# A transformer kernel on one core: another written order at attention's end and through the first two feed-forward samples

## What is computed

```python
h = layernorm(x, gamma1, beta1)
Q = (h @ Wq + bq).reshape(B, T, N_HEADS, D_HEAD).transpose(0, 2, 1, 3)
...
scores = jnp.einsum('bhqd,bhkd->bhqk', Q, K) / np.sqrt(D_HEAD)
scores = jnp.where(causal, scores, -jnp.inf)
attn = jax.nn.softmax(scores, axis=-1)
...
attn_out = ctx @ Wo + bo
x1 = x + attn_out
h2 = layernorm(x1, gamma2, beta2)
ff = jax.nn.gelu(h2 @ W1 + b1, approximate=False) @ W2 + b2
x2 = x1 + ff
g = gate_score[:, None, None]
return x + g * (x2 - x)
```

## Time and profile before

| | |
|---|---|
| median of 3 runs | 1648.11 us (1647.98 to 1650.59) |
| the profiled execution | 1649.63 us, its span 1647.8 us |
| TensorE busy | 1596.5 us, 97% of the span |
| VectorE, ScalarE, GpSimd busy | 1166.0, 980.5, 397.2 us |
| mean granted clock of TensorE | 0.985 of full speed |

### The profile page before, as it was taken

How to read it: one execution, slowest core, us unless ns; L and a number is a source line. 1 busy time by engine, 2 the same in 40 slices (tenths; PEclk the granted TensorE clock), 3 DMA queues, 4 the chain that set the end, 5 groups by cost and what they waited for, 6 DMA issues and landing times.

```text
span 1647.8 us, 27195 instructions
## 1 busy us (share of the span) xinstructions
PE 1596.5 (97%) x9318; PEld 1312.3 (80%) x9318; DVE 1166.0 (71%) x2767; ACT 980.5 (60%) x2329; POOL 397.2 (24%) x606
## 2 busy tenths in 40 slices
PE   5799999999999999999999989999999999999999
PEld 3678777777777777777777668888999999999898
DVE  6799887896868686868678366676565656565643
ACT  5689764987878787878788545343342424242422
POOL 6788800413131313131311110101001020202010
PEclk8999998999999999999999899999999999999999
DMA  7112224544444444444346351866555555646451
GB/s 304 74 77 78 102 91 115 159 115 115 113 120 112 121 112 121 117 116 117 91 98 199 124 220 58 326 238 233 213 205 211 190 219 175 260 151 251 168 205 71
DMA packets 61826, 254.80 MB, mean 155 GB/s; under 512 B 10581, under 2 KB 15957, under 8 KB 45945
## 3 DMA queue, kind: packets, MB, share of 16 engines
q1 hardware_dynamic: 61688, 253.06, 47.1%
HBM read 153.93 MB, written 48.23 MB: 123 GB/s over the span
## 4 chain that ended last, share of the span: by engine, by line
PE 85%; DVE 5%; DMA 4%; ACT 2%; POOL 2%; issue 1%; SPq 1%; DVEq 0%; ACTq 0%; POOLq 0%
PE psum L83 22%; PE psum L84 22%; PE psum L85 21%; PE psum L1647 5%; PE psum L1667 5%; PE psum L1697 4%; DMA k_raw<-in_w_in 1%; DMA k_early<-in_w 1%; PE psum L1588 1%; PE psum L1596 1%; PE psum L1578 1%; PE psum L2597 1%; PE psum L1683 0%; DMA out<-k_result 0%; DMA k_stack<-k_maxima 0%
## 5 line engine op out<-in xcount | busy, mean ns | idle before, releaser
L1347 ACT ACTIVATE psum<-psum,b_mx 128x512 f32<-128x512 f32 (+3 forms) x512 | 258.9, 508 | 64.6 <-DVE b_mx L1094 63.1
L1094 DVE CUSTOM_DVE_ANT_0 psum<-psum,b_mask 128x512 f32<-128x512 f32 (+3 forms) x512 | 244.6, 506 | 54.1 <-PE psum L1647 48.8
L2543 ACT ACTIVATE k_act<-k_stack_f,k_smalls 128x512 f32<-128x512 f32 x112 | 81.0, 723 | 336.1 <-DVE k_stack_f L2381 336.1
L1359 ACT ACTIVATE k_exps<-psum 128x512 f32<-128x512 f32 (+1 forms) x384 | 195.1, 531 | 62.2 <-PE psum L1667 59.5
L968 POOL TENSOR_SCALAR_AFFINE_SELECT k_exps<-k_exps 128x256 f32<-128x256 f32 x256 | 97.2, 417 | 385.8 <-ACT k_exps L1359 385.8
L2360 DVE TENSOR_TENSOR k_act_lo<-k_act,k_act_hi 128x512 fp32r<-128x512 f32 x112 | 77.4, 691 | 130.5 <-ACT k_act_hi L2546 130.5
L2241 POOL TENSOR_SCALAR k_result<-k_result,k_pb 128x512 f32<-128x512 f32 x32 | 58.4, 1840 | 433.5 <-DVE k_result L2300 433.5
L83 PE MATMUL psum<-k_act_hi,k_w_hi 128*128 128x512 f32 x384 | 152.0, 396 | 2.0 <-DVE k_act_lo L2353 1.5
L84 PE MATMUL psum<-k_act_lo,k_w_hi 128*128 128x512 f32 x384 | 151.6, 395 | 0.0
L85 PE MATMUL psum<-k_act_hi,k_w_lo 128*128 128x512 f32 x384 | 151.2, 394 | 0.0
L2381 DVE TENSOR_TENSOR k_raw<-psum,k_raw 128x256 f32<-128x256 f32 x168 | 70.7, 421 | 105.4 <-PE psum L85 99.1
(11 more groups left out here) (377 smaller groups left out, 4411.7 us busy)
## 6 DMA issues: line engine op xcount, KB each, us to landing
k_stack<-w_factors SPq DMA_DIRECT2D x35, 1792.0 KB, 7.9
k_stack<-k_samples SPq DMA_DIRECT2D x384, 128.0 KB, 2.4
k_weights<-w_factors SPq DMA_DIRECT2D x17, 1792.0 KB, 7.7
x<-k_tokens SPq DMA_DIRECT2D x10, 1024.0 KB, 3.9
k_tokens<-x SPq DMA_DIRECT2D x8, 1024.0 KB, 5.3
d<-k_result SPq DMA_DIRECT2D x32, 256.0 KB, 2.9
k_raw<-x SPq DMA_DIRECT2D x8, 1024.0 KB, 4.9
k_raw<-d SPq DMA_DIRECT2D x8, 1024.0 KB, 7.0
```

Source lines behind the costliest of these rows:

```text
L1094: last = dve.tensor_tensor_reduce(got, got, mask[:, S - width:S], -INV_SQRT_DH, -2.0 * MASKED, ALU.add, ALU.min, mx[n % 2][:, h, t:t + 1])
L1347: act.activation(sc(n, u)[:, at:at + width], sc(n, u)[:, at:at + width], ACT.Exp, bias=mx[n % 2][:, h, t:t + 1], scale=-1.0, accum_out=sum ...
L1359: act.activation(exps[n % 2][:, h, at:at + width], by_key(n, u)[:, 0:width], ACT.Exp, scale=INV_SQRT_DH).then_inc(k_act, 1)
L2543: act.activation(act_f[:], whole_tile, ACT.Gelu, bias=small(smalls, "b1", 2 * pair % M + second)).then_inc(pair_gelu, 1)
```

## The change

The four tail functions of SP, VectorE, ScalarE and TensorE get another order. They now reach through sample 1 as well (all of its eight pairs, with pair 8's products, the first of sample 2), so that `samples()` begins with sample 2. The same calls are made with the same arguments. GpSimd's order stays. No wait is added inside a call; only places change. SP's part in full, of the others the pieces at which the text looks (`partial_of`, `finish` and the like of sample 1 are now written in the tail, before they came from `period`):

```diff
 def sync_tail(att, ff):
     att.first_after()
     att.max_rows(29, 1)
     att.stack_rows(31, (0, 1))
+    ff.second_weights(0)
     att.max_rows(30, 0)
     att.attention_out(6, 0)
+    att.stack_rows(31, (2, 3))
+    att.max_rows(30, 1)
     att.attention_out(6, 1)
-    att.stack_rows(31, (2, 3))
     ff.first_weights(0)
-    ff.second_weights(0)
-    att.max_rows(30, 1)
+    att.attention_out(6, 2)
     att.max_rows(31, 0)
-    att.attention_out(6, 2)
+    att.max_rows(31, 1)
+    ff.first_weights(1)
     att.attention_out(6, 3)
-    att.max_rows(31, 1)
     ff.second_weights(1)
     att.attention_out(7, 0)
-    ff.first_weights(1)
-    for k in range(1, 4):
-        att.attention_out(7, k)
     ff.second_weights(2)
+    att.attention_out(7, 1)
+    att.attention_out(7, 2)
     ff.pair_in(2)
+    att.attention_out(7, 3)
     ff.sample_in(1)
+    ff.second_weights(3)
+    ff.pair_in(3)
     ff.factors_out(2)
-    ff.pair_in(3)
-    ff.second_weights(3)
     ff.pair_in(0)
     ff.factors_out(3)
     ff.pair_in(1)
     ff.factors_out(0)
     ff.pair_in(4)
     ff.factors_out(1)
+    ff.factors_in(2)
+    ff.pair_in(5)
+    ff.sample_out(0)
+    ff.factors_out(4)
+    ff.factors_in(3)
+    ff.sample_in(2)
+    ff.factors_in(4)
+    ff.pair_in(6)
+    ff.factors_out(5)
+    ff.factors_in(5)
+    ff.pair_in(7)
+    ff.factors_out(6)
+    ff.factors_in(8)
+    ff.factors_out(7)
...
         def samples():
-            factors_in(2)
-            factors_in(3)
-            pair_in(5)
-            factors_out(4)
-            sample_out(0)
-            factors_in(4)
-            sample_in(2)
-            pair_in(6)
-            factors_out(5)
-            factors_in(5)
-            pair_in(7)
-            factors_out(6)
-            factors_in(HALF)
-            factors_out(7)
             for n in range(HALF + 1, HALF * (B - 1)):
...
 def vector_tail(att, ff):
...
     ff.split(0)
-    ff.w1_low(2)
     att.attention_result(7, 0)
     ff.w2_low(1)
+    att.attention_result(7, 1)
+    ff.split(1)
+    ff.w1_low(2)
+    att.attention_result(7, 2)
     ff.w2_low(2)
-    att.attention_result(7, 1)
-    att.attention_result(7, 2)
-    ff.w2_low(3)
+    ff.w1_low(3)
     att.attention_result(7, 3)
-    ff.split(1)
+    ff.split(2)
     ff.start_result(0)
...
 def scalar_tail(att, ff):
...
+    ff.w2_high(0)
     att.ctx_high(30)
-    att.exponentials_by_key(31, 6)
-    att.exponentials_by_key(31, 7)
-    ff.w1_high(1)
-    ff.w2_high(0)
-    for k in range(8, 12):
+    for k in range(7, 12):
         att.exponentials_by_key(31, k)
     ff.w2_high(1)
+    ff.w1_high(1)
     ff.w2_high(2)
     ff.gelu(0)
...
         def samples():
-            period(0, HALF - 1)
-            for b in range(1, B):
+            for b in range(2, B):
                 for p in range(HALF):
                     period(b, p)
```

More of the change, by code:

```diff
@@ L2706, in samples @@
         def samples():
-            period(0, HALF - 1)
-            for b in range(1, B):
+            for b in range(2, B):
                 for p in range(HALF):
                     period(b, p)
-        return steps(tokens, back, first_product, second_product, samples)
+        return steps(tokens, back, spread, first_product, second_product, product, samples)
     return {"sync": sync, "gpsimd": gpsimd, "vector": vector, "scalar": scalar, "tensor": tensor}
@@ L3092, in vector_tail @@
     att.maxima_out(31, 1)
-    for k in range(3):
+    ff.w1_low(0)
+    for k in range(1, 4):
         att.split_low(k, 8)
-    ff.w1_low(0)
-    att.split_low(3, 8)
     att.ctx_low(30)
@@ L3171, in vector_tail @@
     ff.block_low(1, 2)
+    ff.w2_low(15)
     ff.split(14)
+    ff.split(15)
     ff.block_low(1, 4)
-    ff.factor_low(1, 3)
-    ff.w2_low(15)
-    ff.split(15)
+    ff.factor_low(4, 0)
+    ff.partial_of(0, 0)
+    ff.partial_of(0, 1)
+    ff.factor_low(4, 1)
+    ff.factor_sums(4)
+    for k in range(2, 5):
+        ff.partial_of(0, k)
+    ff.pair_low(0, True)
+    ff.partial_of(1, 0)
+    ff.factor_low(4, 2)
+    ff.finish(0, 0)
+    ff.finish(0, 1)
+    ff.factor_low(4, 3)
+    ff.finish(0, 2)
@@ new lines, in vector_tail @@
+    ff.finish(0, 3)
+    for k in range(1, 4):
+        ff.partial_of(1, k)
+    ff.pair_low(0, False)
+    ff.partial_of(1, 4)
+    ff.partial_of(2, 0)
+    ff.partial_of(2, 1)
+    ff.pair_low(1, True)
+    ff.start_result(1)
+    ff.factor_low(5, 0)
+    ff.factor_low(5, 1)
+    ff.pair_low(1, False)
+    ff.partial_of(2, 2)
+    ff.partial_of(2, 3)
+    ff.factor_sums(5)
+    ff.partial_of(2, 4)
+    ff.partial_of(3, 0)
+    ff.pair_low(2, True)
+    ff.factor_low(5, 2)
+    ff.factor_low(5, 3)
@@ new lines, in vector_tail @@
+    ff.partial_of(3, 1)
+    ff.pair_low(2, False)
+    ff.add_attention(2)
+    ff.partial_of(3, 2)
+    ff.partial_of(3, 3)
+    ff.factor_low(6, 0)
+    ff.pair_low(3, True)
+    ff.partial_of(3, 4)
+    ff.statistics(2, 0)
+    ff.statistics(2, 1)
+    ff.partial_of(4, 0)
+    ff.factor_low(6, 1)
+    ff.factor_sums(6)
+    ff.partial_of(4, 1)
+    ff.statistics(2, 2)
+    ff.pair_low(3, False)
+    for k in range(2, 5):
+        ff.partial_of(4, k)
+    ff.statistics(2, 3)
+    ff.pair_low(4, True)
@@ new lines, in vector_tail @@
+    ff.factor_low(6, 2)
+    ff.partial_of(5, 0)
+    ff.factor_low(6, 3)
+    ff.centre(2)
+    ff.pair_low(4, False)
+    for k in range(1, 4):
+        ff.partial_of(5, k)
+    ff.factor_low(7, 0)
+    ff.normalise(2)
+    ff.partial_of(5, 4)
+    ff.factor_low(7, 1)
+    ff.partial_of(6, 0)
+    ff.pair_low(5, True)
+    ff.partial_of(6, 1)
+    ff.factor_sums(7)
+    ff.block_low(2, 0)
+    ff.partial_of(6, 2)
+    ff.partial_of(6, 3)
+    ff.factor_low(7, 2)
+    ff.block_low(2, 5)
+    ff.pair_low(5, False)
@@ L3179, in scalar_head @@
+    ff.pair_low(8, True)
+    ff.partial_of(8, 4)
 def scalar_head(mod, att):
@@ L3833, in tensor_tail @@
+    att.score_by_key(31, 7)
     ff.first_product(0)
@@ new lines, in tensor_tail @@
+    ff.second_product(22, 7, 2, 3)
+    ff.tokens(2, 2)
+    ff.product(4, 5)
+    ff.product(4, 2)
+    ff.product(4, 3)
+    ff.second_product(23, 6, 0, 1)
+    ff.tokens(2, 3)
+    ff.product(5, 1)
+    ff.product(5, 6)
+    ff.second_product(23, 6, 2, 3)
+    ff.spread(2)
+    ff.product(5, 7)
+    ff.product(5, 4)
+    ff.product(5, 5)
+    ff.second_product(24, 9, 0, 1)
+    ff.second_product(24, 9, 2, 3)
+    ff.product(5, 2)
+    ff.product(5, 3)
+    ff.product(6, 1)
+    ff.product(6, 6)
```

575 lines of the change are left out of this document (369 added, 206 removed).

## The result

The changed kernel takes 1630.07 us (median of 4 runs, 1629.38 to 1630.64), the kernel before 1648.05 beside it (1646.33 to 1650.59): a ratio of 0.9889, 95% interval [0.9872, 0.9907]. The forecast was 1632 within 1626 to 1643. The profiled execution has a span of 1628.8 us.

The account below looks back on a forecast made before the run. TensorE, busy 97%, was taken to bound the kernel, with 23.3 us to be had. Terms 5 + 10 + 2 - 1 = 16 us off the 1647.8 us span gave 1631.8, as a median 1632 us, range 1626 to 1643.

Parts of the forecast that it names:

- What bounds the kernel: TensorE, busy 97% of the span; only its idle time and low clock in three stretches, 23.3 us, could be won.
- First stretch: Attention's end, 900 to 920 us: earlier maxima rows end the stop and clock fall; 5 us, between 1.5 and 8.6.
- the delay of the W2 quarter: Attention's end: the W2 quarter, issued earlier, delays group 30's first maxima; taken as zero, up to 2 us.
- rival B: Attention's end: ScalarE or the W2 quarter holds it, low clock returns, nothing gained there; 1637 or 1642 us, chance 0.20.
- no stop at k_maxima: Sign of being right, 900 to 920 us: TensorE no longer waits for maxima; clock above 0.9, under 2 us idle.
- the walk: Step-by-step timing of the new order, with moved transfers and engine work, to see which stops go and what becomes late.
- the rest: 840 to 900 us and places not walked: reshuffling there can only lose, 0 to 3 us, taken as 1.
- Second stretch: First feed-forward products, 950 to 984 us: earlier transfers and low halves end stops and clock fall; 10 us, bounds 5 and 10.3.
- 0.3 us at the tokens: First feed-forward products: sample 1's load becomes late for TensorE's transposes, the tightest place; taken as 0.3, from 0 to 3 us.
- Third stretch: Pairs of sample 1, 1060 to 1120 us: earlier output store, later result start; 2 us, from 4.3 to a loss of 5.
- Rival D: Sample 1 onward: factor load 4 over 5 us late makes later loads late; slower, 1655 us, chance 0.06.
- Rival C: SP's in-order queue: a held issue holds small transfers behind it, stops return one place later; 1645 to 1651 us, chance 0.06.

Follow-up runs that it names:

- maxima_first: Kernel before, with only the maxima rows of group 30's second half issued ahead of half of W1 and a quarter of W2; 1642.16 us, measured once.
- w1_early: Kernel before, with only the second half of W1 issued earlier, right behind group 31's maxima and ahead of the result stores; 1650.72 us, measured once.
- three_moves: Kernel before, with three SP moves: group 30's second maxima and W1's second half earlier, last W2 quarter with pair load 3 before the first factor store; 1636.44 us.
- third_new: Kernel before, with the new order only through sample 1, from the first pair product on; 1644.72 us, ratio 0.9980.
- third_sp_old: Changed kernel, with SP's order through sample 1 put back as before; 1629.27 us, ratio 0.9893.
- sp_all: Kernel before, with the whole of SP's new order, through sample 1, other engines in their old order; 1634.73 us, ratio 0.9925.
- sum_later: Changed kernel, with group 29's second maxima issued ahead of the 2 MB load and VectorE's first_sum(0) moved later; 1633.64 us, ratio 0.9921.
- sp_new: Kernel before, with SP's new order alone up to the last factor store of sample 0; 1637.24 us, ratio 0.9943.
- heads_old: Changed kernel, with VectorE, ScalarE and TensorE in the old order through attention's end and sample 0; 1631.85 us, ratio 0.9909.
- sp_old: Changed kernel, with SP's old order up to the last factor store of sample 0; 1648.89 us, ratio 1.0005.

## Why the prediction was right, point by point

**What bounds the kernel.** Right: 20.65 us came off TensorE's idle and busy time in the pieces around the three named stretches, of the 23.3 that could be had, and the 500.75 us behind them did not move. That the time came within 2 us of 1632 is in part luck: the terms made 16 us and the pieces 20.65, M came 1.65 us later, and the median lies 1.3 us over the profiled span, not the 0.3 that the forecast added.

**First stretch, 5 us taken, 4.80 measured, but made otherwise.** The transfer was the right one: maxima_first shows that its move alone makes the gain. How it delays was misread: the rows did not need 12.71 us to issue, but 2.57, and then waited behind 3 MB (in the first section). Taking the delay of the W2 quarter as zero held: no stop of TensorE answers to it. What was wrong is how the 5 us were made up. I took them from ScalarE's load (3.2 at 83% busy, 6.9 never idle) and counted idle time and clock alike; in fact 4.07 are clock and 0.73 idle. Little of the idle time was given back: 1.85 of 4.31 us stayed in 900 to 920, and a stop of 1.74 us came at 883. ScalarE is busy 20.97 us of 23.60 (89%), above the 83% that I allowed it. It is what was late next, as forecast, if only by little: TensorE's stop of 0.50 us at 907.75 is for its copy (k_tokens), and the one of 0.96 us at 910.45 for maxima that VectorE could not finish before ScalarE's logarithms:

```profile
910.04 0.36 DVE L1174 TENSOR_TENSOR b_mx<-b_mx,b_logs 128x8 f32<-128x8 f32 x1 [1.24 <-ACT b_logs L1392]
```

These stops did not bring the low clock, and so rival B's first half falls. The sign that I named, "no stop at k_maxima", holds in 900 to 920, for which it was named; the one that is left is group 29's, 20 us earlier, and the walk had not looked there. That is where "the rest" of -1 us went: 2.10 - 0.37 = 1.73 us from 840 to 900. With it the forecast for the piece was 5 - 1 = 4, against 4.80.

**Second stretch, 10 us taken, 10.44 measured.** Each of the named stops went, and all of the clock's 3.4 us. The walk left 0.3 us at the tokens; nothing was lost there. The half of W1 is borne out by itself: without its move the stop is 3.48 us (maxima_first), with it 1.03 (w1_early). The pair load is not: the tokens' stop stays with the W1 half moved alone, at 2.38 us, and is gone in three_moves, but it is 0.99 us in third_new and gone in maxima_first, and neither of these moves that load. Its move alone wasn't tried. The low halves' and the token copy's new places, on which the walk also counted, were not needed: three_moves has none of them and lacks 0.84 us of this piece.

**Third stretch, 2 us taken, 5.41 measured: the term that was mis-sized, and for a wrong reason.** I put the gain on SP (the output's store ahead of the store of factors) and took half of it off again for late factor loads. third_sp_old shows that SP's order is not needed at all. With the engines' own order the partial sums come before TensorE wants them, whether VectorE waits for the store or not. third_new shows that the order ahead of Q has a part in it: with the old one 2.5 us are gained behind Q and not 5.4. The upper end of 4.3 was too low as well, as it was TensorE's idle time: busy time went down by 1.65 us for the same 712 matmuls. A part of that lies in how a stop is recorded: the last matmul before one is drawn with its whole 0.39 us, where the next would start 0.23 us later, so each stop costs 0.16 us more than its idle row; four stops fewer are 0.6 us. The remaining 1.0 us I can't place.

**Rival D, the late factor load.** In the kernel after load 3 goes out at 1032.99, 17 us after Q, and load 4 at 1042.86, 27 us after: about the 1.6 and 2.5 periods of the walk. They took 11.5 and 11.8 us to land, longer than the 9.7 of the earlier trace rows, and both were in time. The one that was late, by 0.6 us, is load 5. Factor loads of 840 to 1120 into k_stack took 9.4 us in the median of the kernel after, near the 9.7 of the earlier trace rows; the 6.2 us by estimate from the Trainium skill, "DMA: Bandwidth & Descriptors" (Anatomy of one DMA), don't hold in this queue. The mechanism itself is real: sp_all paid 1.95 us and a fall of the clock to it, and third_new 1.60 us, for the very load 4 that the forecast named. One has the old order of the other engines throughout, the other the old order of all engines up to Q; the forecast could have seen this as a condition.

**Rival C** falls with the waits of the kernel after: the stops did not come back one place later, but for the 1.7 us at 883.

## What to carry to other kernels

Before rewriting the order of four engines, look for the small transfer that is queued behind megabytes: three moved issues in one queue gave 0.65 of the 1.11% here, and the engines' new order through the same stretches nothing without them, and with them less than could be measured. Read next to each stop the clock, since most of the first gain was a clock that no longer fell; removing one microsecond of idle time brought five. When a big load is moved back, list both who wants it and what is queued behind it; sum_later failed on the second list.

## What the hardware showed that I had not expected

**Equal stops, unequal clock.** In sp_new and heads_old TensorE has the same work and the same stops at attention's end. Three of its waits in sp_new, then in heads_old:

```profile
904.18 0.51 PE L1667 MATMUL psum<-k_stack 98*128 98x384 f32 x2 [0.95 <-ACT k_exps L1359]
908.27 0.39 PE L1667 MATMUL psum<-k_stack 98*128 98x256 f32 x1 [0.65 <-ACT k_exps L1359]
909.23 1.71 PE L1697 MATMUL psum<-k_exps,k_result 128*32 128x512 f32 x16 [0.58 <-POOL k_exps L968]
```

```profile
904.64 0.50 PE L1667 MATMUL psum<-k_stack 98*128 98x384 f32 x2 [0.96 <-ACT k_exps L1359]
908.73 0.39 PE L1667 MATMUL psum<-k_stack 98*128 98x256 f32 x1 [0.65 <-ACT k_exps L1359]
909.69 2.37 PE L1697 MATMUL psum<-k_exps,k_result 128*32 128x512 f32 x16 [0.57 <-POOL k_exps L968]
```

These stops agree to 0.01 us, yet in heads_old the 16 matmuls behind them take 2.37 us instead of 1.71, and the granted clock of 910 to 915 is 0.66, a mix of 2.4 and 1.2 GHz, against 1.00 over the whole of 900 to 920 in sp_new. It costs 1.7 us from M to C. maxima_first, three_moves and sp_all have these stops too, and no fall. The Trainium skill, "TensorE: Matmul & The Clock Gate" (Part 1), says of the slow matmuls at a kernel's start that their number is run-variable. No run here was read for the start; these traces show such a difference in the middle of a kernel. I take it that this order sits near a fall; whether one that spreads the stops has more margin isn't shown.

**A long stop without a fall, and with one.** In the kernel before the longest stop, the 3.43 us at 955.44, left the clock at 1.00; it fell behind the next, shorter ones (2.35 and 1.47 us at 972.88 and 975.00). The table by stretch of the kernel before:

```profile
950.00:957.00 7.00, 3.57 (x16) 2.64 (x15) 4.45 (x7) 3.61 (x7) 6.65 (x4) 1.00 0.91 338
957.00:972.00 15.00, 13.52 (x63) 10.67 (x61) 9.25 (x16) 6.19 (x12) 0.00 (x0) 1.00 0.66 246
972.00:984.00 12.00, 9.66 (x31) 7.67 (x32) 7.30 (x13) 5.77 (x10) 0.00 (x0) 0.72 0.10 30
```

In third_new it was the other way round: behind its stop of 3.69 us at the same place the mean clock of 957 to 972 is 0.89, and that of 972 to 984 is 1.00. In maxima_first it is 0.50 from 951 to 956, behind a stop of 3.48 us. The length of a stop alone doesn't tell whether the clock falls, so I would not price one from its length.

**A tiny transfer is issued as fast as ever, and lands late.** Four rows of maxima took 2.42 to 2.90 us to issue in every set of 870 to 915 us, before and after, with 3 MB ahead of them too. But behind 3 MB they reached TensorE 9.6 us after their issue began before (893.90 to 903.52) and 9.5 us in sp_old (896.52 to 906.01). A timeline row that joins several issues of a queue also spans the queue's wait between them, so a long one is to be looked at in a narrower window.
